# Quantised FFN weight tiles: transposed on TensorE and copied by ScalarE, or transposed by a DMA

## What is computed

```python
q, k, v = LN(x) @ Wq / sqrt(HD), ctx @ Wk, ctx @ Wv      # x, ctx: (16, 256, 512); 16 heads of 128
x = x + softmax(q k^T) v @ Wo
# per block of 32 values along the last axis:
scale = 2 ** (floor(log2(max|w|)) - 2);  q_w(w) = clip(round_to_4_bits(w / scale), +-6) * scale
gate, up = q_act(LN(x)) @ q_w(w_gate).T, q_act(LN(x)) @ q_w(w_up).T
x = x + q_act(silu(gate) * up) @ q_w(w_down).T            # w_gate, w_up: (2048, 512); w_down: (512, 2048)
```

## Time and profile before

| what | value |
|---|---|
| median of 3 executions | 2310.7 us (2306.71 to 2312.22) |
| the profiled execution's own time | 2307.97 us |
| its span in the trace | 2306.4 us |
| granted TensorE clock, mean | 0.991 of full speed |
| instructions | 51300 |

### The profile page before, as it was taken

The page is one execution under the profiler, slowest core; times in us unless marked ns, Lnnn a source line. Parts: engine busy times, 40 slices in busy tenths (PEclk is TensorE's granted clock), DMA queues, the critical chain, the costliest instruction groups (busy, mean ns, idle before and its releaser), DMA issues.

```text
span 2306.4 us, 51300 instructions
## 1 busy us (share of the span) xinstructions
PE 2138.5 (93%) x16458; PEld 1555.5 (67%) x16458; DVE 1636.6 (71%) x3487; ACT 1135.3 (49%) x3016; POOL 778.4 (34%) x1156
## 2 busy tenths in 40 slices
PE   6999999999999999999999999999998888888887
PEld 5677777777777777777777777777886433333333
DVE  6766666666666666666666666655554699999998
ACT  7754444444454444444444444544444444454443
POOL 4322222222232222222222222211100367666674
PEclk9999999999999999999999999999999999999999
DMA  6723323232323232333332333232324211111111
GB/s 221 184 64 74 78 63 83 65 79 64 80 63 79 65 79 60 79 67 79 65 82 64 79 64 80 54 70 60 58 58 115 78 52 53 55 50 50 55 50 46
DMA packets 321374, 170.75 MB, mean 74 GB/s; under 512 B 277504, under 2 KB 290304, under 8 KB 321216
## 3 DMA queue, kind: packets, MB, share of 16 engines
q1 hardware_dynamic: 304720, 129.81, 25.5%
q0 software_dynamic: 10320, 32.25, 4.6%
q10 hardware_dynamic: 6176, 6.29, 0.9%
HBM read 77.86 MB, written 23.07 MB: 44 GB/s over the span
## 4 chain that ended last, share of the span: by engine, by line
PE 53%; DVE 26%; issue 10%; DMA 5%; ACT 5%; DVEq 1%; POOL 0%; POOLq 0%; SPq 0%; ACTq 0%
PE b_qk L1038 18%; PE b_v L1038 11%; PE b_w L1148 6%; PE b_c L1038 6%; PE b_s L1038 6%; DMA probT<-psplit 5%; PE b_o L1148 4%; DVE psplit L818 4%; DVE attn_weights L950 3%; ACT psplit L590 3%; DVE attn_weights L965 3%; DVE attn_weights L955 3%; DVE ffn_amax L761 2%; DVE x_amax L880 1%; DVE rsum L812 1%
## 5 line engine op out<-in xcount | busy, mean ns | idle before, releaser
L582 ACT ACTIVATE prob<-b_s,nmax 128x256 f32<-128x256 f32 x514 | 238.8, 469 | 510.3 <-DVE nmax L802 509.8
L818 DVE SCALAR_TENSOR_TENSOR psplit<-prob,rrec,psplit 128x256 f16<-128x256 f32 x514 | 252.8, 533 | 266.1 <-ACT psplit L590 266.1
L1038 PE MATMUL b_qk<-xT,attn_weights 128*128 (+1 forms) x3072 | 379.9, 274 | 0.0
L1038 PE MATMUL b_v<-attn_weights,kvT 128*128 128x256 f16 x3072 | 378.6, 273 | 0.0
L1038 PE MATMUL b_qk<-kvT,attn_weights 128*128 (+1 forms) x3072 | 377.8, 273 | 0.0
L590 ACT ACTIVATE psplit<-prob,rrec 128x256 f16<-128x256 f32 x514 | 233.2, 500 | 226.1 <-DVE rrec L815 223.7
L1038 PEld LDWEIGHTS b_qk<-xT,attn_weights 128*128 128x128 f16 x3072 | 301.5, 98 | 36.3
L1038 PEld LDWEIGHTS b_v<-attn_weights,kvT 128*128 (+1 forms) x3072 | 301.1, 98 | 35.5
L1038 PEld LDWEIGHTS b_qk<-kvT,attn_weights 128*128 128x128 f16 x3072 | 300.8, 98 | 35.4
L802 DVE TENSOR_REDUCE nmax<-b_s 128x2 f32<-128x512 f32 x257 | 177.0, 689 | 116.1 <-PE b_s L1038 115.9
L391 POOL DMA_DIRECT2D kvrow<-kvt x61 | 34.7, 569 | 628.5 <-DVE kvT L727 628.5
(11 more groups left out here) (133 smaller groups left out, 3197.4 us busy)
## 6 DMA issues: line engine op xcount, KB each, us to landing
ffn_w<-wffn SPq DMA_DIRECT2D x48, 256.0 KB, 2.7
acc<-xtok POOLq DMA_DIRECT2D x16, 512.0 KB, 4.3
x_tiles<-x_scratch SPq DMA_DIRECT2D x32, 256.0 KB, 2.7
attn_weights<-x_scratch SPq DMA_DIRECT2D x32, 256.0 KB, 2.6
out<-attn_weights SPq DMA_DIRECT2D x32, 256.0 KB, 2.0
xrow<-xq POOLq DMA_DIRECT2D x61, 128.0 KB, 2.5
kvrow<-kvt POOLq DMA_DIRECT2D x61, 128.0 KB, 2.3
x_scratch<-acc POOLq DMA_DIRECT2D x15, 512.0 KB, 3.3
```

The lines of the kernel that those rows point to most:

```text
L582: last = eng.activation(half(prob, q, 256), half(bS, q, 256), ACT.Exp, bias=nmax[:, q:q + 1], scale=1.0, accum_out=rsum[:, q:q + 1])
L818: last = eng.scalar_tensor_tensor(out=p_part(k, q, 1), in0=half(prob, q, 256), scalar=rrec[:, q:q + 1], in1=p_part(k, q, 0), op0=ALU.mult, ...
L1038: last = eng.matmul(out, l, r, start=(a == 0), stop=(a == len(pairs) - 1))
```

## The change

TensorE's four transposes of a weight tile and ScalarE's copy out of the PSUM bank go, with their semaphore `ffn_tr` and the name `pW` of the bank. In their place SyncE issues one DMA transpose from `wb` to `wt`, in slot 0 behind transpose_p, and the store moves from slot 0 to slot 1, behind that slot's transpose_p and ahead of the load. Before the new transpose SyncE waits for `ffn_q` of the tile and for the store of the tile before, and the store waits for the landing of the transpose. GpSimd's last step (L438) waits for the landing of the transpose of the tile before, where it waited for TensorE's.

```diff
+            def transpose_ffn(w):
+                wait_apart(eng, "ffn_q", w + 1)
+                if not isinstance(w, int) or w > 0:
+                    wait_apart(eng, "ffn_stored", 16 * w)
+                eng.dma_start_transpose(wt[:, :].rearrange("p (c f) -> p c f", c=4), wb[:, :]
+                                        ).then_inc(sm["ffn_moved"], 16)
+
             def store_ffn(w):
-                eng.wait_ge(sm["ffn_moved"], w + 1)
+                eng.wait_ge(sm["ffn_moved"], 16 * (w + 1))
                 eng.dma_start(wqs[bass.ds(w, 1), :, :].rearrange("g p f -> p (g f)"), wt[:, :]
                               ).then_inc(sm["ffn_stored"], 16)
...
                 for k in range(QUAD):
                     transpose_p(4 * n + k, k % 2)
                     if store and k == 0:
+                        transpose_ffn(n - FFN_FROM - 1)
+                    if store and k == 1:
                         store_ffn(n - FFN_FROM - 1)
...
-                eng.wait_ge(sm["ffn_tr"], w)
+                eng.wait_ge(sm["ffn_moved"], 16 * w)
                 eng.tensor_tensor(grid(wb[:, :]), grid(wr), spread(ws), ALU.mult).then_inc(sm["ffn_q"], 1)
...
-                    if ffn and k == 0:
-                        w = n - FFN_FROM - 1
-                        eng.wait_ge(sm["ffn_tr"], w + 1)
-                        if not isinstance(w, int) or w > 0:
-                            eng.wait_ge(sm["ffn_stored"], 16 * w)
-                        eng.activation(wt[:, :], pW, ACT.Copy).then_inc(sm["ffn_moved"], 1)
...
-                    if ffn and k == 0:
-
-                        w = n - FFN_FROM - 1
-                        eng.wait_ge(sm["ffn_q"], w + 1)
-                        if not isinstance(w, int) or w > 0:
-                            eng.wait_ge(sm["ffn_moved"], w)
-                        for c in range(4):
-                            last = eng.transpose(pW[:, c * P:(c + 1) * P], wb[:, c * P:(c + 1) * P], identb[:, :])
-                        last.then_inc(sm["ffn_tr"], 1)
```

More of the change, by code:

```diff
@@ L171, in build @@
                                             ("b_s", "b_qk", "b_c", "b_v", "b_pt", "b_o", "b_x", "b_w")]
-        pW = bPT[:, 0:256].bitcast(BF16)
         o_bank = [bO, bW]
@@ L189, in build @@
             ffn_loaded ffn_amax ffn_pow ffn_scale ffn_inv ffn_y ffn_exp ffn_magic ffn_add ffn_sub ffn_clip ffn_q
-            ffn_tr ffn_moved ffn_stored gate_up_resident down_resident
+            ffn_moved ffn_stored gate_up_resident down_resident
             tile_loaded res_loaded t_sum t_mean t_square t_step t_rstd t_xn
```

## The result

The changed kernel takes 2343.67 us (median of 4, 2342.06 to 2347.14) against 2309.41 us for the kernel before (median of 4): a ratio of 1.0149 (95% interval 1.0136 to 1.0163), 34 us slower. I had forecast no difference.

The account below looks back on a forecast made before the run. The prediction took VectorE's chain in slot 0, not TensorE, to bound the kernel where the transposes stand. Terms -1.2 + 0 + 0, about -1 us, took the median 2310.7 to 2309.7 us, range 2303 to 2322.

Parts of the forecast that it names:

- What is taken away: Step pricing the work removed from TensorE and ScalarE in slot 0: 8 x 0.15 = 1.2 us gained, the copy nothing.
- A second-order term: Instruction-queue packets coming later in TensorE's shorter list, beside probability transposes: taken as zero, between -1 and +12 us.
- the 0.16 given to slower: Chance of a slower kernel: 0.10 for rival C with a rival that the change misbehaves, 0.06 for Rival D.
- TensorE's transposes are worth nothing, since VectorE's chain ends last: Slot 0: 0.22 us less TensorE work gives nothing in 40 quads waiting for VectorE, about 0.15 us in 8 others.
- the wait for the lo part: TensorE's wait before slot 1's scores for VectorE's lo part of the projections, forecast to grow from 22.4 to 31 us.
- ScalarE's copy is covered: In slot 0 the 0.60 us copy is followed by 1.65 us of idle time, so removing it gains nothing.
- The new transpose is covered on SyncE: Issued in 1.24 us, landing in 3.1, off the queue 2.6 us before slot 1's probability transpose: costs nothing.
- It doesn't harm the probability transpose ahead of it: Slot 0's probability transpose, with 0.6 us slack, still lands in 3.1 us, the new transfer 1.5 us behind: cost 0.
- rival C: New transpose delays slot 0's probability transpose to 4.6 us, 0.9 us a quad, 43 us: 2354; 0.10, shared with another rival.
- Rival B: TensorE is the bound after all, so 0.22 us is gained in all 48 quads, 10.6 us: 2300; chance 0.07.
- Rival D: Instruction-queue packets fall on slot 0 at batch edges, late probability transposes costing 1.1 us each, up to +12: 2322; chance 0.06.

Follow-up runs that it names:

- Run 2: The kernel before with 221 counting instructions at the start of TensorE's list, its work untouched: 2374.93 us, ratio 1.0280.
- run 1: The changed kernel with 35 counting instructions at the start of TensorE's list: 2306.68 us, ratio 0.9986 to the kernel before.
- run 9: The changed kernel with 9 counting instructions at the start of TensorE's list: 2311.04 us, ratio 1.0009 to the kernel before.
- runs 3 and 4: The changed kernel with TensorE's four transposes kept too: 2312.61 us; the changed kernel with 35 counting instructions and a plain DMA copy for the DMA transpose: 2307.42 us.
- run 10: The changed kernel with TensorE's loop over quads 9 to 52 written out: 2316.14 us, ratio 1.0035 to the kernel before.
- runs 5 and 9: The changed kernel with 8 and with 9 counting instructions at the start of TensorE's list: 2350.25 us (ratio 1.0165) and 2311.04 us (ratio 1.0009).
- runs 7 and 8: The changed kernel with 215 and with 170 counting instructions at the start of TensorE's list: 2337.0 and 2330.1 us, one execution each.
- run 11: The kernel of run 10 with 90 counting instructions ahead of the second tile of the FFN part: 2327.93 us, ratio 1.0076 to the kernel before.

## Why the prediction was wrong

The step that failed is in "What is taken away", and its continuation in "A second-order term". I priced the instructions removed by their time on the engine, and followed what their absence does to the packets of the instruction queue only as traffic beside the probability transposes. I did work out that the packets come at other moments. I didn't ask what happens when TensorE itself waits for one: that term stood at nothing without a reason, and it measured 3.35 us a pass, 33 us in ten. The kernel before had no such wait at the scores, because its loop happens to start early in a piece, by the edge found above 26 instructions into one: 35 instructions were removed ahead of it, the edge came to 9 instructions into the loop, and after each branch back TensorE then waits for two pieces one behind the other. Run 2 shows the loss with the old work at the new place, runs 1 and 9 the new work without it. As none of my cases held a cost outside the quad's semaphores and queues, the range (2303 to 2322) missed, and the 0.16 given to slower was all given to other mechanisms.

Point by point:

- *TensorE's transposes are worth nothing, since VectorE's chain ends last.* Right. In the quad shown, output projection to slot 1 scores is now 25.78 - 23.87 = 1.91 us, forecast 1.90; the wait for the lo part, forecast at 31 us, is 32.5 in run 1. With the loop in its place the change gains 3 us (0.14%) where I said 1, but runs 1 and 9 differ by 4 us with the same work, so the term can't be told from zero. In the trace I count nine quads at 1.29 to 1.32 us and 39 with a wait, where the prediction has 8 and 40; that changes the term by 0.15 us.
- *ScalarE's copy is covered.* Right: ScalarE has 48 instructions fewer, and that shows nowhere in the chain.
- *The new transpose is covered on SyncE.* Right. It takes 1.19 us to issue (I took 1.24), lands in 2.4 us in the median (I took 3.1), and SyncE waits neither for `ffn_q` nor for `ffn_stored`.
- *It doesn't harm the probability transpose ahead of it* (rival C). Right: 3.1 us to landing in the quad shown as in the earlier trace rows, and runs 3 and 4. Rival C had nearly the right time, 2354, by the wrong mechanism; the time alone would have "confirmed" it, had the row of waits for probT not fallen.
- *Rival B* falls with the waits of run 1. *Rival D* is a real mechanism, as run 10 shows, but smaller than I had it (0.5 us of waiting a quad for the 1.1 I gave), and it played no part in the change: the row of waits for probT fell.

A smaller point on the same step: of the 3.4 us that a pass loses, about 2.6 are the stop and the rest is the granted clock, 0.80 over the 6 us that follow.

The fastest version is run 1, 0.14% under the kernel before; with run 9 beside it, that is no gain to count on.

## What to carry to other kernels

Instructions taken out of an engine's list move every loop behind them against the pieces in which the list is brought. If a time moves by much more than the instructions weigh, look for idle time "issue" at a fixed place of a loop body, in the midst of a group without a wait, and try the same kernel with some counting instructions ahead of the loop, before any theory of engines or queues. An empty instruction isn't free, though: put such padding where the engine waits anyway, and measure more than one amount.

## What the runs showed of the hardware that I had not expected

- One instruction ahead of a loop made 36 to 39 us in 2311 (runs 5 and 9), by 115.1 - 111.3 = 3.8 us a pass. The stop is longest with the edge just behind the loop's first instructions (4.5 us each with 1 or 2 left, some of it in the place of the wait for VectorE), 2.6 us with 9 left, 0.8 us with 50, none with 95.
- Counting instructions on TensorE took about 0.16 us each in a long row, (37.00 - 29.93) / 45 from runs 7 and 8, and 13.3 us for 90 in run 11, far more than the 0.06 us between the instructions of a pass (111.4 us for 1972).
- Writing the loop out didn't help: run 10 is 7 us slower than the kernel before, which has its loop in a good place. The cause is open.
- Behind a stop of 2.8 us, with TensorE busy 0.79 of 4 us, the granted clock was 0.80 on average over 6 us, half speed for some 3.3 us of them and full speed for the rest, at a cost of about 1 us.
